# Attention on one core: two key blocks of the exponentials are added on VectorE before the row totals, the gate comes from tanh, and ScalarE copies the turned keys

## What is computed

```python
Q = normalize((x @ W_q.T).reshape(b, t, 16, 4));  K = normalize((x @ W_k.T).reshape(b, t, 16, 4))
V = (x @ W_v.T).reshape(b, t, 16, 64)
Qn = normalize(einsum('bthd,hde->bthe', Q, W_nudge))
scores = einsum('bqhd,bkhd->bhqk', Qn, K) * 0.5
s = sigmoid(3.0 * einsum('bthd,rd->bthr', K, simple_roots))          # the gate
cw = prod(s[..., None, :] * bits + (1 - s[..., None, :]) * (1 - bits), axis=-1)
scores = scores + einsum('bthc,hc->bth', cw, chamber_bonus)          # one bonus per key
attn = softmax(where(causal, -inf, scores))                          # exp, row totals, division
out = einsum('bhqk,bkhv->bqhv', attn, V).reshape(b, t, 1024) @ W_out.T
```

## Time and profile before

| | |
|---|---|
| median of 3 runs | 1770.89 us (1768.71 to 1771.26) |
| profiled execution | 1770.72 us, its span 1769.0 us |
| mean granted TensorE clock | 0.971 |
| attention | about the first 770 us of the span |

### The profile page before, as it was taken

One profiled execution on the slowest core, in us unless ns is written; L12 is line 12 of the kernel. 1 busy time (PEld: TensorE's weight loads), 2 busy tenths in 40 slices (PEclk: granted clock), 3 DMA queues, 4 the chain that ended last, 5 costly groups with the idle time before them and its releaser, 6 DMA issues.

```text
span 1769.0 us, 47120 instructions
## 1 busy us (share of the span) xinstructions
PE 1650.8 (93%) x14871; PEld 1237.2 (70%) x14871; DVE 1317.2 (74%) x3869; ACT 889.0 (50%) x2003; POOL 1000.8 (57%) x1782
## 2 busy tenths in 40 slices
PE   5999999999999999849999999999999999789996
PEld 3677777777777777537788888777787886555553
DVE  5588888888888888745567777777777775748886
ACT  2666666666666666514444444444444442224443
POOL 7788888888888888712223333333333333227777
PEclk9999999999999999969999999999999999689998
DMA  1011111111111113010110000000000002434441
GB/s 42 11 50 55 51 49 50 50 49 51 53 54 54 54 54 104 14 36 25 60 60 31 31 31 31 22 30 23 28 30 29 25 25 99 155 116 134 134 131 41
DMA packets 78259, 95.96 MB, mean 54 GB/s; under 512 B 7046, under 2 KB 62995, under 8 KB 78160
## 3 DMA queue, kind: packets, MB, share of 16 engines
q1 hardware_dynamic: 70992, 77.91, 13.9%
q0 software_dynamic: 7168, 16.87, 2.7%
HBM read 53.14 MB, written 43.69 MB: 55 GB/s over the span
## 4 chain that ended last, share of the span: by engine, by line
PE 39%; DVE 8%; issue 5%; POOL 2%; DMA 1%; ACT 1%; DVEq 0%; POOLq 0%; SPq 0%; ACTq 0%
PE main L1371 6%; PE main L1373 5%; PE main L1380 5%; PE main L1529 3%; PE yp L1451 3%; PE main L1311 2%; PE xi L1286 2%; PE main L1435 2%; PE main L1324 2%; PE main L1438 1%; PE main L1436 1%; PE route L1543 1%; PE xi L1543 1%; PE turn L1279 1%; POOL out L1269 1%
## 5 line engine op out<-in xcount | busy, mean ns | idle before, releaser
L662 ACT ACTIVATE wgu<-score 128x384 f32<-128x384 f32 x512 | 223.2, 490 | 80.2 <-PE score L484 78.8
L1371 PE MATMUL main<-hT_high,h_high 128*128 128x512 f32 x512 | 221.2, 432 | 0.9 <-ACT hT_high L1628 0.9
L1373 PE MATMUL main<-hT_high,h_low 128*128 128x512 f32 x512 | 201.3, 393 | 0.0
L506 PE MATMUL outp<-wgu 128*32 128x256 f32 (+1 forms) x4096 | 196.3, 333 | 3.3 <-POOL wgu L327 2.2
L327 POOL TENSOR_SCALAR_AFFINE_SELECT wgu<-wgu 128x512 f32<-128x512 f32 x256 | 166.4, 655 | 52.0 <-ACT wgu L662 34.3
L506 PEld LDWEIGHTS outp<-wgu 128*32 128x32 f32 x4096 | 116.6, 111 | 69.5 <-issue 23.3
L1380 PE MATMUL main<-hT_low,h_high 128*128 128x512 f32 x512 | 138.3, 391 | 0.1
L1936 DVE SCALAR_TENSOR_TENSOR th<-th,main 128x512 f32<-128x512 f32 x64 | 43.9, 685 | 115.2 <-ACT th L1655 115.2
L544 PE MATMUL back<-wout,wgu 128*128 128x128 f32 x1024 | 128.6, 280 | 0.0
L544 PEld LDWEIGHTS back<-wout,wgu 128*128 128x128 f32 x1024 | 121.8, 195 | 0.4
L1269 POOL DMA_INDIRECT out<-res,idx x96 | 96.7, 1008 | 44.3 <-issue 40.7
(11 more groups left out here) (295 smaller groups left out, 4361.4 us busy)
## 6 DMA issues: line engine op xcount, KB each, us to landing
sorted_d<-row_buf SPq DMA_DIRECT2D x26, 772.0 KB, 3.7
xg<-sorted_d SPq DMA_DIRECT2D x48, 386.0 KB
wgu<-in_gate_up SPq DMA_DIRECT2D x4, 2048.0 KB
xa<-in_x SPq DMA_DIRECT2D x32, 128.0 KB, 3.4
xr<-in_x SPq DMA_DIRECT2D x32, 128.0 KB, 3.2
x_d<-x SPq DMA_DIRECT2D x32, 128.0 KB, 1.8
x1c<-x_d SPq DMA_DIRECT2D x16, 256.0 KB, 2.8
x1v<-x_d SPq DMA_DIRECT2D x16, 256.0 KB, 2.7
```

The lines of the kernel that those rows point to most:

```text
L506: m = pe.matmul(outp[AUG * j:AUG * (j + 1), p % 2, k * P:T], val[par][:, k, h, v:v + AUG], weights(h, k), start=(k == 0), stop=(k == 1), t ...
L662: act.activation(prob[:, h // 2 % (RING // 2), :, h % 2, :], score[h % BANKS][:, 0:SC].rearrange("p (c q) -> p c q", q=P), ACT.Exp).then_i ...
L1371: pe.matmul(main[m % 2][:, :], w[0][:, k, m * P:(m + 1) * P], src[0][:, k, :], start=(k == 0), stop=False)
L1373: pe.matmul(main[m % 2][:, :], w[1][:, k, m * P:(m + 1) * P], src[0][:, k, :], start=False, stop=False)
```

## The change

The column sums of queries 128 to 255 run over two key blocks. Before, TensorE took both through the selecting matrix. Now VectorE adds blocks 1 and 2 of a group's four heads (`fold`, a 128x512 addition with both inputs in SBUF, four in a round), and TensorE takes the sum through the matrix (`folded_totals`, one group late, and the last group's at once). The reciprocal waits for the last of these (`p_fold`), and an exponential that reuses a place in the ring waits for `folded` besides. The gate is 0.5 tanh(1.5x) + 0.5: ScalarE computes Tanh in the place of Exp, and VectorE's reciprocal goes. ScalarE copies the turned keys in VectorE's place. The running maximum reads the turned bonus in the accumulator with a constant `lowest` as its other input, without the copy `bonT`. On VectorE `input_norm` now stands ahead of the sum `x1`.

```diff
-        bonT = sb("bonT", [HEADS, T])
+        lowest = sb("lowest", [HEADS, T])
...
+        folded = sb("folded", [P, 2, GH, P])
...
+                const(pool.memset(lowest[:], -3.4028234663852886e38))
...
+            def folded_totals(b, g):
+
+                wait(pe, s["folded"], GROUPS * b + g + 1)
+                for j in range(GH):
+                    m = pe.matmul(total[AUG * j:AUG * (j + 1), P:T], pick[:, g, :], folded[:, g % 2, j, :],
+                                  start=False, stop=(g == GROUPS - 1), tile_position=(0, AUG * j),
+                                  skip_group_check=True)
+                m.then_inc(s["p_fold"], 1)
...
-                for k in range(2):
-                    for j in range(GH):
-                        m = pe.matmul(total[AUG * j:AUG * (j + 1), k * P:T], pick[:, g, :],
-                                      weights(GH * g + j, k), start=(g == 0 and k == 0),
-                                      stop=(g == GROUPS - 1 and k == 1), tile_position=(0, AUG * j),
-                                      skip_group_check=True)
+                for j in range(GH):
+                    h = GH * g + j
+                    m = pe.matmul(total[AUG * j:AUG * (j + 1), 0:P], pick[:, g, :],
+                                  prob[:, h // 2 % (RING // 2), 0, h % 2, :], start=(g == 0), stop=(g == GROUPS - 1),
+                                  tile_position=(0, AUG * j), skip_group_check=True)
                 m.then_inc(s["p_sum"], 1)
+                if g > 0:
+                    folded_totals(b, g - 1)
+                if g == GROUPS - 1:
+                    folded_totals(b, g)
...
                     wait(act, s["p_sum"], GROUPS * b + (h - RING) // GH + 1)
+                    wait(act, s["folded"], GROUPS * b + (h - RING) // GH + 1)
...
-                    act.activation(ek[:], fr[:, :, 1], ACT.Exp, scale=-3.0).then_inc(s["ek"], 1)
+                    act.activation(ek[:], fr[:, :, 1], ACT.Tanh, scale=1.5).then_inc(s["ek"], 1)
...
                 weights(b, 14, 15)
                 if f is not None:
+                    wait(act, s["p_kaT"], f + 1)
+                    wait(act, s["p_score"], HEADS * (f - 1))
+                    act.activation(k_augT[1 - par][:].rearrange("p g t -> p (g t)"), turned_b[:, :],
+                                   ACT.Copy).then_inc(s["kaT"], 1)
...
-                wait(dve, s["p_sum"], GROUPS * (z + 1))
+                wait(dve, s["p_fold"], GROUPS * (z + 1))
...
+            def fold(b, g):
+                if b is None:
+                    return
+                wait(dve, s["masked"], PAIRS_A * b + 2 * g + 2)
+                wait(dve, s["p_fold"], GROUPS * b + g - 1)
+                first = 2 * g % (RING // 2)
+                dve.tensor_tensor(folded[:, g % 2].rearrange("p (r i) q -> p r (i q)", i=2),
+                                  prob[:, first:first + 2, 1].rearrange("p r i q -> p r (i q)"),
+                                  prob[:, first:first + 2, 2].rearrange("p r i q -> p r (i q)"),
+                                  ALU.add).then_inc(s["folded"], 1)
...
-                    dve.tensor_scalar(ek1[:], ek[:], 1.0, None, ALU.add).then_inc(s["ek1"], 1)
+                    dve.tensor_scalar(sg[:], ek[:], 0.5, 0.5, ALU.mult, ALU.add).then_inc(s["sg"], 1)
...
-                    dve.wait_ge(s["ek1"], n + 1)
-                    dve.reciprocal(sg[:], ek1[:]).then_inc(s["sg"], 1)
...
                 reciprocal(z)
+                fold(b, 0)
...
                 normalise(z, par, 0)
+                fold(b, 1)
...
-                    dve.tensor_copy(bonT[:], turned[0:HEADS, 0:T]).then_inc(s["bonT"], 1)
-                    dve.wait_ge(s["bonT"], f + 1)
                     wait(dve, s["p_cmax"], f)
-                    dve.tensor_tensor_scan(out=cmax[0:HEADS, :], data0=bonT[:], data1=bonT[:], initial=bonT[:, 0:1],
+                    dve.tensor_tensor_scan(out=cmax[0:HEADS, :], data0=lowest[:], data1=turned[0:HEADS, 0:T],
+                                           initial=lowest[:, 0:1],
                                            op0=ALU.max, op1=ALU.max).then_inc(s["cmax"], 1)
...
-                if f is not None:
-                    wait(dve, s["p_kaT"], f + 1)
-                    wait(dve, s["p_score"], HEADS * (f - 1))
-                    dve.tensor_copy(k_augT[1 - par][:].rearrange("p g t -> p (g t)"), turned_b[:, :])\
-                       .then_inc(s["kaT"], 1)
...
                 normalise(z, par, 3)
+                fold(b, 2)
...
+                input_norm(m)
+                fold(b, 3)
+                if y is not None:
                     dve.wait_ge(s["yn"], y + 1)
...
                     dve.tensor_tensor(x1[:], yn[:], xr[:], ALU.add).then_inc(s["x1"], 1)
-                input_norm(m)
```

More of the change, by code:

```diff
@@ L143, in attention_layer @@
         ek = sb("ek", [P, TT, HEADS, DH])
-        ek1 = sb("ek1", [P, TT, HEADS, DH])
         sg = sb("sg", [P, TT, HEADS, DH])
@@ L195, in attention_layer @@
         names = ("w_qk", "w", "const", "xa", "stat_a", "mv_a", "ve", "rstd", "xn", "p_xnT", "xnT", "p_qk", "sq1", "ss1",
-                 "ssg1", "roots", "qkn", "p_qkT", "qkT", "p_rot", "sq2", "ek", "qraw", "ss2", "ssg2", "ek1",
-                 "sg", "q4", "kcopy", "bon", "p_bonT", "bonT", "cmax", "p_cmax", "q5", "ksplit", "qsplit", "kaug",
-                 "qaug", "p_kaT", "p_qaT", "kaT", "qaT", "p_v", "val", "p_score", "prob", "masked", "p_out", "raw",
+                 "ssg1", "roots", "qkn", "p_qkT", "qkT", "p_rot", "sq2", "ek", "qraw", "ss2", "ssg2",
+                 "sg", "q4", "kcopy", "bon", "p_bonT", "cmax", "p_cmax", "q5", "ksplit", "qsplit", "kaug",
+                 "qaug", "p_kaT", "p_qaT", "kaT", "qaT", "p_v", "val", "p_score", "prob", "masked", "folded", "p_fold", "p_out", "raw",
                  "p_sum", "rec", "rec_high", "rec_rest", "rec_mid", "rec_parts", "rest_row", "wv_split", "low_sel", "back_row", "back_r", "xnT_high", "xnT_low", "p_bc", "onT", "p_y",
@@ L206, in attention_layer @@
         N_IDENT = 4
-        N_CONST = 22
+        N_CONST = 23
         ctx.callback(clear, nc, list(s.values()))
```

## The result

The changed kernel takes 1797.61 us in the median (1795.52 to 1800.23), the kernel before 1769.8 beside it: a ratio of 1.0158, 95% interval 1.0143 to 1.0174. It is slower by 28 us. The profiled execution took 1795.52 us, its span 1793.8.

What follows compares the result with a forecast made beforehand. TensorE bounded the kernel before; VectorE's loop through `qkn` was expected to bound it after: 10.87 + 2.15 + 10.15 = 23.17 us against 22.32. Over 28 rounds, 28 x 0.85 = 24 us on 1770.72 gave 1795 us, range 1760 to 1820.

Steps and rivals of the forecast that it cites:

- TensorE's saving, 0.89 us a round: In the totals, 512 of a group's 768 columns remain: 0.22 us saved a group, 0.89 us a round.
- VectorE's bill: Four additions of 128x512 on VectorE, each 0.83 us on its path, with bounds 0.62 and 1.22 us.
- Reciprocal to `qkn`: First stretch of VectorE's loop, lengthened by the first and second additions: 9.21 + 2 x 0.83 = 10.87 us.
- `qkn` to the turn of the keys: Second stretch: TensorE's 1.94 us, 0.1 for the signal, 0.1 for a later spreading, together 2.15 us.
- Turn of the keys to the reciprocal: Last stretch: TensorE's arm 9.94 us, VectorE's 9.9; taken as 10.15 with GpSimd's `rstd` put off by the third addition.
- My own test for this: Sign at VectorE's wait for `rstd`: it should be under 0.5 us a round, from 1.14 before.
- The second rival, GpSimd becomes the bound: Additions hold GpSimd up by 0.38 us each: round 22.9 us, kernel 1788 us; chance 0.15.
- The sign that I had named for it: GpSimd has no wait for ScalarE left, and masks hold TensorE up.
- What was said to cost nothing: Keys' copy on ScalarE, 1.02 us, fits 2.13 us of idling; tanh brings no table load into the round.
- the two loops: VectorE's through `qkn` and the turn of the keys, 23.17 us, chance 0.58; GpSimd's with holds, 22.9 us, chance 0.15.

Runs made afterwards that it cites:

- e2: Changed kernel without the additions, TensorE taking the totals over 128 columns twice, one key block left out: ratio 0.9883 to the kernel before, round 21.72 us.
- e1: Changed kernel without VectorE's additions, totals through the matrix over both key blocks as before: ratio 0.9986 to the kernel before, round 22.30 us.
- e4: Changed kernel with the second addition of a round moved behind `q5` on VectorE: ratio 1.0197 to the kernel before, round 23.55 us.
- e6: Changed kernel with only the third and fourth groups summed on VectorE, by additions, the first two through the matrix: ratio 1.0096 to the kernel before.
- e5: Changed kernel with only the third and fourth groups summed on VectorE, by one-input reductions, the first two through the matrix: ratio 1.0009 to the kernel before.
- e7: Changed kernel with GpSimd's 1.02 us power replaced by a subtraction, giving wrong scales: ratio 1.012 to the kernel before, round 23.00 us.
- e10: e5 with GpSimd's copy of the normalised keys moved to ScalarE: ratio 0.9999 to the kernel before, round 22.37 us.
- e11: e10 with the fourth group's sum moved ahead of `xn` on VectorE: 1763.24 us, ratio 0.9973 to the kernel before, round 22.18 us.
- e3: Changed kernel with all four additions replaced by one-input reductions giving the same sums: ratio 1.0285 to the kernel before.
- e8: Changed kernel with the second addition behind `q5` and GpSimd's power replaced by a subtraction: 1776.29 us, ratio 1.0047 to the kernel before, round 22.66 us.

## Why the prediction came out

The time (1795 forecast, 1797.61 measured) and the sign were right. The mechanism was right in part, and the part that sets the round was the rival. The nearness of the number is luck: 10.87 + 2.15 + 10.15 = 23.17 was forecast, about 10.5 + 2.05 + 10.7 = 23.24 measured, an error of 0.4 one way and one of 0.55 the other.

- **TensorE's saving, 0.89 us a round.** Nearly right: without the columns TensorE is busy 0.80 us a round less (e2 against e1), and the kernel is 1.2% faster. Only 0.59 arrives even with no bill at all.
- **VectorE's bill, 0.83 us for an addition** (0.82 by its own terms, 0.69 - 0.07 + 0.2). Too high ahead of `qkn`, 0.74 and 0.60, and too low for the fourth addition, 1.15 from start to start (316.36 to 317.51); the median instruction took 0.81 us. Reciprocal to `qkn` was forecast as 10.87 us and measured as 10.37.
- **"`qkn` to the turn of the keys", 2.15.** Measured 2.04 (328.65 to 330.69).
- **"Turn of the keys to the reciprocal", 10.15.** The step that failed. It took 341.90 - 330.69 = 11.21 us in this round. `qkn` comes 10.37 or some 10.6 us in, in turn from round to round, so with the mean round of 23.24 the mean of this leg is 23.24 - 10.5 - 2.05 = 10.7. I let `rstd` come 6.3 us behind the turn and the reciprocal 3.54 behind that, and allowed some 0.3 for all delay of `rstd` "put off by the third addition". Measured, `rstd` ends 6.6 and 7.5 us behind the turn in two rounds one after the other (turns at 307.97 and 330.69, `rstd` at 314.58 and 338.20), and the reciprocal follows 3.70 behind each. GpSimd is late by the holds; that they are those of all four additions and not of the third alone is argued from its busy time. My own test for this failed as well: VectorE's wait for `rstd` was to fall under 0.5 us and doubled to 2.2.
- **The second rival, GpSimd becomes the bound.** Forecast with 0.15: four holds of 0.38 us. Measured: 0.38 each (e1), and the round follows GpSimd's busy time up and down (e4 +0.31 for +0.31; e6 against e5 +0.44 for +0.45) until another loop stops it (e7). I had the rival's price right and gave it a low chance because a gap might hide the holds; that it is right to the hundredth is chance, since the forecast took the largest delay of one instruction and e1 gives a mean of totals. Its sum, 22.9, lacks the waits for others: GpSimd's round without them went from 21.6 to 22.6 us, and 0.6 of waits remain. The sign that I had named for it was half met: GpSimd's waits for exponentials fell from 19.7 to 13.4 us and did not vanish.
- **What was said to cost nothing.** Shown by e1: tanh, the keys' copy and the scan are free together, and no table load came into the rounds.
- **Not tested.** In the changed kernel TensorE stands at the head of its queue before an addition's sum, 12.3 us in 28 rounds (L494). In the half version with the copy moved, an earlier fourth sum was worth 0.19 us a round (e10, e11); with all four additions no run moves it, so it may hold a share of the 0.93 us beside GpSimd's own work.

The Trainium skill (SBUF — State Buffer, "Who interferes with whom") says that VectorE's instructions with two SBUF inputs and GpSimd's reads exclude each other, and that a reduction never contends. The runs agree in direction: GpSimd is busy 1.53 us a round more with four additions (e1 against the changed kernel), and 73.27 / 4 - 17.96 = 0.36 more with four reductions (e3). Whether the 0.36 comes from the reductions or from other instructions of VectorE that they shifted no run shows; if it is the shift, an addition's own hold is nearer (1.53 - 0.36) / 4 = 0.29 us. Either is less than the instruction's 0.81, so in the mean not its whole length.

With the two loops this close (23.24, and 23.0 in e7) a number built on the wrong one can come out right. It would not have told anyone what to mend: shortening VectorE's way to `qkn` (e4) made the kernel slower.

## What to carry to other kernels

When the chains of several engines are nearly as long as the round (here 22.3 us on TensorE and 21.6 on GpSimd), an instruction moved to one of them must be priced on the others too, in work and in what it blocks: here 0.8 us given to VectorE cost GpSimd 0.38, and GpSimd was the engine that could not pay. A longer instruction that blocks less (a reduction with one input, 1.24 us) can be worth more than a shorter one that blocks more (1.01), as long as its own engine has the time: with half of the sums it was (e5, e6), with all four the reductions made the slower kernel (e3 1.0285, the additions 1.0158). And a wait at the head of TensorE's queue holds up the scores behind it (0.19 us a round between e10 and e11): issue such a sum when its operand is surely there, or produce the operand ahead of work that is less urgent.

## What the runs showed of the hardware

- An addition of 128x512 with both inputs in SBUF held GpSimd up by 0.38 us in the mean (e1 against the changed kernel; 0.29 if the 0.36 us a round that GpSimd gained with four reductions is taken off); the same sums as a reduction of 128x1024 over strided pairs took 1222 to 1250 ns, hardly varying, where the additions varied from 677 to 1230.
- A relief of 1 us on GpSimd, which waited 0.6 us a round for others, moved the round by 0.24 us (e7). The late addition cost 0.31 us in one kernel and gained 0.34 in the next (e4, e8).
